# Flag 2 summed behind the fourth chunk, tile 2 normalised by GpSimd, and new orders for every engine

## The chip, the core and the metric

One core of a Trainium2 chip runs the whole program. The metric is the device time of one execution in microseconds. The kernel before was timed three times: 368.39, 368.41 and 369.13 us, median 368.41.

## The reference, cut to what matters

The input is 16 sequences of 256 tokens with 128 features, 4096 tokens. It goes through a feed-forward block (FFN), an attention-like block, and the same FFN again, each with a residual.

```
ln(x)  = (x - mean) / sqrt(var + 1e-5)                 # over the 128 features
ffn(x) = h = silu(x @ w1.T * s1) * (x @ w2.T * s2)     # 128 -> 512, weights of -1, 0, 1
         h = gelu(h @ h1.T * sh1); h = gelu(h @ h2.T * sh2)   # 512 -> 512, exact gelu
         return h @ w3.T * s3                          # 512 -> 128
att(x) = h = ln(x) * gamma + beta
         keys = h @ Wk.T + bk; values = h @ Wv.T + bv
         w = exp((keys @ Wka.T + bka) / sqrt(128)); w = w / cumsum(w)   # along the sequence
         return cumsum(w * keys) * values
x = x + 0.5 * ffn(ln(x));  x = x + att(ln(x));  x = x + 0.5 * ffn(ln(x))
```

## The kernel before, in words

**Tiles and stages.** The 4096 tokens are 8 tiles of 512. Each FFN works on each tile, so there are 16 tiles of FFN work: T = 0 to 7 are the first FFN, 8 to 15 the second, and a0 to a7 are the attention of a tile. Activations stand with features on partitions and the 512 tokens along the free axis. In the order strings, p1.m is hidden chunk m (of 4) of w1 and w2 (two banks of PSUM: "gate" and "up"), p2.m and p3.m are chunk m of h1 and h2, p4 is w3. tanh, gate and up form the gated product of chunk m; high1, high2 and high3 round an activation to a high part, low1, low2 and low3 form the remainder; gelu2 and gelu3 belong to p2 and p3. Each product is made twice, with the high and with the low part, as one weight block of 128x128 against 512 columns: 16 matmuls for p1 of a tile, 32 for p2, 32 for p3, 8 for p4.

**Orders.** START, SECOND_LAYER and STEPS (lines 27 to 186) hold, for each engine, the order of its instructions, written out by hand. Each step of STEPS is one tile; AHEAD (line 193) says how many tiles ahead of the step an item without a number works; "2:t" is item t of tile 2. Engines meet through semaphores alone: every instruction waits for the counts that it needs, and what stands behind it in its engine's order waits with it.

**Flags.** The weights are exact in the high format if their low bits are zero. DVE and ACT reduce the low bits of each part of the weights (items bits:...), raise_flag gathers them (line 1015), TensorE sums them over the partitions with a one-column matmul (flag_sum, line 750), copy_flag brings the sum to SBUF as an integer (line 1024), and TensorE loads it into a register and takes one of two copies of the following instructions (lines 851 to 860). Flag 1 (w1, w2) stands ahead of p1 of tile 0; flag 2 (h1) ahead of the second layer of tile 0; flag 3 (h2, w3) ahead of the rest. Before, flag 2 is summed between p1.1 and p1.2 of tile 0 in the bank y_ps, and p1.3, which writes that bank, waits for its copy (line 684). In the second layer of tile 0 (p2_first, line 698) the products run chunk by chunk of their input (a, b, c, d), hi and lo, into four banks at once, as the inputs come.

**Norms.** Tiles 0 to 2 (BY_PE, line 189) are normalised with the tokens on partitions: DVE takes statistics (norm_stats, norm_aggr, norm_veps), GpSimd takes the root (norm, line 575), ACT writes z (z_blocks), and TensorE turns z by four transposes (item t on PE, line 785) into PSUM. ACT and DVE read it from there as xn_hi and xn_lo. The other tiles are normalised "over columns": DVE takes the statistics, GpSimd aggregates them (aggregate, line 533) into a small tile of means and roots, SyncE's queue writes it to memory (park, line 488) and reads it back broadcast to all partitions in two transfers (wide, line 497), and GpSimd adds and multiplies the tile's columns (xn_add and xn_mult, items xn.0 and xn.1). TensorE isn't needed for it.

**Loads.** SyncE's queue issues the weights and the first tiles' x, waits for h2 and w3, then loads x of tiles 2 to 7 (x_sb), four attention weights, and xt, the transposed input, in one transfer (lines 481 to 486).

Of the kernel before, what the change touches and what calls it, by code (L numbers as in the profile page):

```python
# [29 lines left out]
        "p1.0 p1.1 flag:sum2 p1.2 p1.3",  # L30
    ),
    "ACT": (
        "hi:w1 hi:w2 z",
        "t vec:s1 bits:h1.1 bits:h1.3 tanh.0 tanh.1 tanh.2 high1.0 tanh.3 high1.1 z.0 z.1 high1.2 bits:h2.0 "
        "high1.3 1:t",
    ),
    "DVE": (
        "stats aggr veps bits:w1 bits:w2 norm",
        "flag:copy1 bits:h1.0 t vec:scales bits:h1.2 stats flag:raise2 aggr gate.0 veps flag:copy2 up.0 gate.1 "
        "up.1 low1.0 gate.2 up.2 gate.3 up.3 bits:h2.1 low1.3 1:t",  # L40
# [11 lines left out]
        "",  # L52
        "park wide",
        "a0:park a0:wide park wide",
        "a1:park park a1:wide wide",
        "park wide",
        "a2:park park a2:wide wide",
# [5 lines left out]
        "a6:park 8:store a6:wide park wide",  # L63
        "a7:park a7:wide 9:store park wide",
        "10:store park 11:store wide store",
# [4 lines left out]
        "norm",  # L70
        "norm xn.0 xn.1",
        "a0:norm norm a0:xn.0 a0:xn.1 xn.0 xn.1",
        "a1:norm norm a1:xn.0 a0:weight a1:xn.1 xn.0 xn.1",
        "norm a0:dt xn.0 xn.1",
        "a2:norm a1:weight norm a2:xn.0 a2:xn.1 a1:dt xn.0 xn.1",
        "a3:norm norm a3:xn.0 a3:xn.1 a2:weight xn.0 xn.1",
        "a2:dt norm a4:norm xn.0 xn.1",
        "a3:weight norm a4:xn.0 a4:xn.1 xn.0 xn.1",
        "a5:norm a3:dt a4:weight a5:xn.0 a5:xn.1 norm a4:dt xn.0 xn.1",
# [68 lines left out]
    ),  # L148
    "DVE": (
# [36 lines left out]
}  # L186

POOL_FIRST = ("norm", 1, 2)
BY_PE = (0, 1, 2)
AGGREGATE = 3  # L190
LINES = 4

# [4 lines left out]
def macaron_block(nc, x, xt, w1t, w2t, h1t, h2t, w3t, wkt, wkat, wvt, wkn, vecs, out, seq):  # L197
# [10 lines left out]
    with ExitStack() as ctx:  # L208
# [219 lines left out]
        def flag_home(part):  # L428
            return (hid_ps[0], y_ps, xt_ps)[part - 1][0:1, 0:1]
# [93 lines left out]
        def _(eng):  # L523
# [79 lines left out]
            for k in range(MC):  # L603
                hi("h2", k)
# [613 lines left out]
```

## Time and profile before

| what | value |
|---|---|
| median of three runs | 368.41 us |
| the profiled execution's own time | 368.15 us |
| its span, first to last instruction | 366.4 us |
| TensorE's mean granted clock | 0.998 |
| busy: TensorE, DVE, ACT, GpSimd | 98%, 86%, 77%, 45% |
| read and written | 18.36 and 2.18 MB |

Times in the rows are microseconds from the start of the span. PE is TensorE, DVE VectorE, ACT ScalarE, POOL GpSimd, and SPq the transfers that SyncE issues. A timeline row gives the start, the busy time, the engine, the line, the operation, output<-input, the shapes and, in brackets, the idle time before it and what ended it. The end of a matmul is modelled: a 512-column matmul shows 0.39 us while the next one starts 0.23 us behind it.

### The profile page before, as it was taken

What the parts mean: (1) busy time and instruction counts of PE and PEld (TensorE: products, weight loads), DVE (VectorE), ACT (ScalarE), POOL (GpSimd) and SP (SyncE); (2) the same over time, 40 slices, a digit from 0 to 9 for tenths busy, and PEclk for the clock granted to TensorE, in tenths of its full rate; (3) what the DMA queues carried; (4) which work ended last, traced back from release to release, by engine and by line L of the source; (5) the groups of instructions that cost most, each with busy time, mean ns of one, the idle gap of its engine ahead of it and who ended that gap; (6) DMA issues with size and microseconds to landing.
All of it is one profiled execution on the core that took longest, in us unless ns stands there. A gap on an engine that the chain in (4) does not pass through costs nothing.

```text
span 366.4 us, 5194 instructions
## 1 busy us (share of the span) xinstructions
PE 359.3 (98%) x1578; PEld 285.1 (78%) x1578; DVE 316.2 (86%) x550; ACT 283.1 (77%) x465; POOL 163.3 (45%) x251
## 2 busy tenths in 40 slices
PE   7999999999999999999999999999999999999996
PEld 2678888787877777788778787787778777888885
DVE  5999688999989998889899989998899799857642
ACT  4998777987777879776887968877897697686763
POOL 3553344649045565812685545652573740530000
PEclk9999999999999999999999999999999999999999
DMA  7770103030100301300222012012022020040001
GB/s 245 270 294 4 54 3 107 8 110 9 58 2 0 86 29 36 83 0 2 59 59 59 1 59 59 0 59 86 0 59 88 2 86 2 4 111 2 1 30 63
DMA packets 16256, 20.94 MB, mean 57 GB/s; under 512 B 7008, under 2 KB 8288, under 8 KB 15968
## 3 DMA queue, kind: packets, MB, share of 16 engines
q1 hardware_dynamic: 15504, 19.75, 18.2%
q10 hardware_dynamic: 720, 0.80, 0.7%
q8 instruction: 16, 0.26, 0.3%
q14 instruction: 16, 0.13, 0.1%
HBM read 18.36 MB, written 2.18 MB: 56 GB/s over the span
## 4 chain that ended last, share of the span: by engine, by line
PE 96%; DVE 2%; issue 1%; ACT 1%; POOL 0%; POOLq 0%; ACTq 0%
PE hid_ps L643 62%; PE gate_ps L643 8%; PE y_ps L643 8%; PE up_ps L643 7%; PE y_ps L662 2%; PE xt_ps L829 2%; PE xt_ps L833 2%; PE xt_ps L836 2%; PE y_ps L843 1%; PE gate_ps L707 1%; PE up_ps L707 1%; DVE gate L1070 0%; PE xt_ps L643 0%; DVE xt_sb L1142 0%; PE xt_ps L656 0%
## 5 line engine op out<-in xcount | busy, mean ns | idle before, releaser
L643 PE MATMUL hid_ps<-act_hi,hi_h 128*128 128x512 f32 x480 | 193.3, 403 | 0.0
L643 PE MATMUL hid_ps<-act_lo,hi_h 128*128 128x512 f32 x480 | 186.7, 389 | 0.0
L1092 DVE TENSOR_TENSOR act_lo<-full,act_hi 128x512 fp32r<-128x512 f32 x185 | 132.8, 742 | 23.6 <-ACT act_hi L909 20.6
L902 ACT ACTIVATE full<-hid_ps,vec 128x512 f32<-128x512 f32 x123 | 84.1, 687 | 57.2 <-PE hid_ps L643 51.7
L643 PEld LDWEIGHTS hid_ps<-act_hi,hi_h 128*128 128x128 f32 x480 | 90.3, 188 | 22.8 <-issue 2.6
L643 PEld LDWEIGHTS hid_ps<-act_lo,hi_h 128*128 128x128 f32 x480 | 90.2, 188 | 21.3 <-issue 2.6
L909 ACT ACTIVATE act_hi<-full 128x512 fp32r<-128x512 f32 x127 | 78.6, 628 | 1.6
L567 POOL TENSOR_TENSOR xnt<-xt_sb,wide 128x512 f32<-128x512 f32 x21 | 29.4, 1400 | 45.8 <-DMA wide<-rows 45.8
L885 ACT ACTIVATE tanh<-gate_ps,s_half 128x512 f32<-128x512 f32 x60 | 40.4, 680 | 7.4 <-PE gate_ps L643 7.3
L1070 DVE SCALAR_TENSOR_TENSOR gate<-tanh,gate_ps 128x512 f32<-128x512 f32 x60 | 40.3, 674 | 6.5 <-ACT tanh L885 6.4
L1082 DVE SCALAR_TENSOR_TENSOR full<-up_ps,s_half,gate 128x512 f32<-128x512 f32 x60 | 44.1, 741 | 1.1
L890 ACT ACTIVATE act_hi<-full 128x512 fp32r<-128x512 f32 x60 | 36.9, 625 | 1.9 <-DVE full L1082 1.7
L573 POOL TENSOR_TENSOR xnt<-xnt,wide 128x512 f32<-128x512 f32 x21 | 30.0, 1428 | 3.2 <-POOL xnt L567 0.4
L622 POOL TENSOR_TENSOR xt_sb<-xt_sb,adelta 128x512 f32<-128x512 f32 x8 | 12.3, 1532 | 42.7 <-DVE adelta L1174 42.7
L540 POOL TENSOR_TENSOR pair_diff<-stats 128x4 f32<-128x4 f32 x21 | 8.2, 388 | 44.2 <-DVE stats L1040 44.2
L1158 DVE RECIPROCAL rcsum<-csum 128x256 f32<-128x256 f32 x16 | 27.8, 1740 | 0.0
L553 POOL TENSOR_TENSOR pair<-veps,half 128x4 f32<-128x4 f32 x21 | 26.1, 1244 | 3.3 <-POOL veps L550 0.4
L643 PE MATMUL gate_ps<-xn_hi,hi_w 128*128 128x512 f32 x59 | 25.1, 425 | 0.3 <-ACT full L902 0.3
L643 PE MATMUL y_ps<-act_hi,hi_w 128*128 128x512 f32 x60 | 23.8, 396 | 0.0
L643 PE MATMUL y_ps<-act_lo,hi_w 128*128 128x512 f32 x60 | 23.4, 390 | 0.0
L643 PE MATMUL gate_ps<-xn_lo,hi_w 128*128 128x512 f32 x59 | 23.0, 391 | 0.0
L643 PE MATMUL up_ps<-xn_hi,hi_w 128*128 128x512 f32 x59 | 23.0, 390 | 0.0
(170 smaller groups left out, 440.3 us busy)
## 6 DMA issues: line engine op xcount, KB each, us to landing
wide<-rows SPq DMA_DIRECT2D x42, 256.0 KB, 3.7
xt_sb<-xt SPq DMA_DIRECT2D x1, 2048.0 KB, 10.6
out<-xt_sb SPq DMA_DIRECT2D x7, 256.0 KB, 4.0
x_sb<-x SPq DMA_DIRECT2D x1, 1536.0 KB, 6.8
raw_h<-h2t SPq DMA_DIRECT2D x4, 256.0 KB, 7.1
raw_h<-h1t SPq DMA_DIRECT2D x2, 256.0 KB, 6.1
rows<-pair SPq DMA_DIRECT2D x21, 4.0 KB, 2.2
raw_w<-w2t ACTq DMA_DIRECT2D x1, 256.0 KB, 4.0
```

The costliest lines, as they stand in the source:

```text
L553: eng.tensor_tensor(pair_b[q][:, 1, :], veps[:, :], half[:, :], ALU.pow).then_inc(s_pow, 1)
L567: eng.tensor_tensor(xnt_b[i][:, :], xt_tile(t), wide_b[i][:, 0:TOK], ALU.add).then_inc(s_centred, 1)
L573: eng.tensor_tensor(xnt_b[i][:, :], xnt_b[i][:, :], wide_b[i][:, TOK:2 * TOK], ALU.mult).then_inc(s_xn, 1)
L643: mm = eng.matmul(ps, w, a, start=(first and n == 0), stop=(last and n == len(seq_) - 1))
L885: eng.activation(tanh_b[m % 2][:, :], gate_home(T, m)[:, :], ACT.Tanh, scale=s1_half[:, m:m + 1]).then_inc(s_tanh, 1)
L890: eng.activation(act_hi[first_act(T)][:, m, :], full1[m % 2][:, :], ACT.Copy).then_inc(s_hi[1], 1)
L902: eng.activation(full23[m % 2][:, :], home23(n, T, m)[:, :], ACT.Gelu, scale=col("sh1" if n == 2 else "sh2", m)).then_inc(s_gelu[n], 1)
L909: eng.activation(act_hi[n][:, m, :], full23[m % 2][:, :], ACT.Copy).then_inc(s_hi[n], 1)
L1070: eng.scalar_tensor_tensor(gate_b[m % 2][:, :], tanh_b[m % 2][:, :], 1.0, gate_home(T, m)[:, :], ALU.add, ALU.mult).then_inc(s_gate, 1)
L1082: eng.scalar_tensor_tensor(full1[m % 2][:, :], up_home(T, m)[:, :], s12_half[:, m:m + 1], gate_b[m % 2][:, :], ALU.mult, ALU.mult).then_in ...
L1092: eng.tensor_tensor(act_lo[a][:, m, :], full[m % 2][:, :], act_hi[a][:, m, :].bitcast(F32), ALU.subtract).then_inc(s_lo[n], 1)
L1158: eng.reciprocal(rcsum[:, b], csum[:, b]).then_inc(s_rc, 1)
```

## The change

Flag 2: its sum moves behind p1.3 of tile 0 into the bank gate_ps[0], and waits for gate.0 instead of xn_lo. p1.3 no longer waits for the copy. Tile 2 leaves BY_PE: its four transposes, z and root are gone, and it is normalised over columns. Its rows and its columns of xt get transfers of their own with two semaphores, ahead of the rest. On GpSimd the casts of h2 and w3 become items of the order, three casts of h2 ahead of tile 2's aggregation, the fourth behind it, w3 behind xn.1. All orders are written anew. On ACT the reductions of h1's bits move from ahead of tanh.0 to between the tanhs. In the diff below the steps 2 to 15 of each engine, which hold the same items as before in other orders, are left out.

```diff
 START:
     "PE": (
         "flag:sum1 t",
-        "p1.0 p1.1 flag:sum2 p1.2 p1.3",
+        "p1.0 p1.1 p1.2 p1.3 flag:sum2",
     "ACT": (
-        "hi:w1 hi:w2 z",
-        "t vec:s1 bits:h1.1 bits:h1.3 tanh.0 tanh.1 tanh.2 high1.0 tanh.3 high1.1 z.0 z.1 high1.2 bits:h2.0 "
-        "high1.3 1:t",
+        "hi:w1 hi:w2 z 0:t vec:s1",
+        "tanh.0 tanh.1 bits:h1.1 tanh.2 bits:h1.3 bits:h2.0 high1.0 tanh.3 high1.1 z.0 high1.2 z.1",
     "DVE": (
-        "stats aggr veps bits:w1 bits:w2 norm",
-        "flag:copy1 bits:h1.0 t vec:scales bits:h1.2 stats flag:raise2 aggr gate.0 veps flag:copy2 up.0 gate.1 "
-        "up.1 low1.0 gate.2 up.2 gate.3 up.3 bits:h2.1 low1.3 1:t",
+        "stats aggr veps bits:w1 bits:w2 norm flag:copy1 0:t bits:h1.0 vec:scales",
+        "bits:h1.2 gate.0 stats up.0 aggr flag:raise2 gate.1 flag:copy2 veps up.1 low1.0 gate.2 up.2 gate.3 "
+        "up.3 2:stats low1.3 1:t bits:h2.1 bits:h2.2 flag:raise3 1:gate.0 flag:copy3 1:up.0 0:low2.0 0:low2.1 "
+        "1:gate.1 1:up.1 3:stats 0:low2.2 0:low2.3 1:gate.2 1:low1.0 1:up.2",
 SECOND_LAYER:
-    "p2ahi.0 p2ahi.1 p2ahi.2 p2ahi.3 p2alo.1 p2alo.3 p2bhi.3 p2alo.0 p2alo.2 p2bhi.0 p2bhi.2 t p2blo.0 p2bhi.1 "
-    "p2blo.1 p2blo.3 p2chi.0 p2blo.2 p2clo.0 p2dhi.0 p2chi.1 p2chi.2 p2clo.1 p2dlo.0 p2chi.3 p2dhi.1 p2clo.3 "
-    "p2clo.2 p2dlo.1 flag:sum3 p1.0 p2dhi.2 p2dhi.3 p1.1 p2dlo.2 p2dlo.3"
+    "p2ahi.2 p2ahi.1 p2ahi.3 p2alo.2 p2alo.3 p2alo.1 p2ahi.0 p2bhi.0 p2bhi.1 p2bhi.2 p2alo.0 p2blo.1 p2blo.0 "
+    "p2chi.0 p2chi.1 p2blo.2 t p2clo.1 p2clo.3 p2dhi.1 p2clo.0 p2dhi.0 p2chi.2 p2dlo.0 p2dhi.3 p1.0 p2bhi.3 "
+    "p2dlo.1 p2clo.2 p2blo.3 p2dhi.2 flag:sum3 p2chi.3 p2dlo.2 p2dlo.3 p1.1"
 STEPS, steps 0 and 1:
     "SP": (
-        "",
+        "park wide",
     "POOL": (
-        "norm",
-        "norm xn.0 xn.1",
+        "hi:h2.0 hi:h2.1 hi:h2.2 norm hi:h2.3 xn.0 xn.1",
+        "hi:w3 norm xn.0 xn.1",
     "PE": (
-        "p1.2 p1.3 fold p3.0 p3.1",
-        "t 0:p3.2 p1.0 0:p3.3 p2.0 p1.1 p2.1 p2.2 p2.3 p4 p1.2 p1.3 a0:u p3.0 p3.1 p3.2 p3.3",
+        "p1.2 fold p1.3 p3.0 p3.1 p3.2 p3.3",
+        "p1.0 p1.1 p2.0 p2.1 p4 p2.2 p2.3 p1.2 a0:u p1.3 p3.0 p3.1 p3.2 p3.3",
     "ACT": (
-        "bits:w3 bits:h2.3 gelu2.0 high2.0 gelu2.1 tanh.0 high2.1 tanh.1 gelu2.2 gelu2.3 high2.2 high1.0 "
-        "high2.3 high1.1 tanh.2 z gelu3.0 tanh.3 2:t high3.0 gelu3.1 high1.2 high3.1 gelu3.2 high1.3 high3.2 "
-        "gelu3.3 high3.3",
+        "0:high1.3 bits:w3 t bits:h2.3 gelu2.0 tanh.0 gelu2.1 high2.0 high2.1 tanh.1 gelu2.2 gelu2.3 high2.2 "
+        "tanh.2 high2.3 tanh.3 high1.0 high1.1 gelu3.0 gelu3.1 high1.2 high3.0 2:t high3.1 gelu3.2 high3.2 "
+        "2:tanh.0 high1.3 gelu3.3 high3.3",
     "DVE": (
-        "bits:h2.2 flag:raise3 stats low2.0 flag:copy3 aggr gate.0 veps low2.1 gate.1 up.0 up.1 low2.2 low2.3 "
-        "fold low1.0 gate.2 3:stats up.2 low1.1 2:t gate.3 up.3 low3.0 low1.2 low3.1 low1.3 low3.2 low3.3",
+        "low1.1 gate.3 low3.0 2:t up.3 low3.1 low1.2 low1.3 2:gate.0 low3.2 fold",
...
-BY_PE = (0, 1, 2)
-AGGREGATE = 3
+BY_PE = (0, 1)
+AGGREGATE = 2
...
+        s_x2t, s_xt2 = sem("s_x2t"), sem("s_xt2")
...
-        norm_of = {("ffn", t): t for t in range(2)}
-        for i, order in enumerate(STEPS["DVE"]):
+        norm_of = {}
+        for i, order in enumerate(START["DVE"] + STEPS["DVE"], -2):
...
-            return (hid_ps[0], y_ps, xt_ps)[part - 1][0:1, 0:1]
+            return (hid_ps[0], gate_ps[0], xt_ps)[part - 1][0:1, 0:1]
...
-            xload(2, NT, s_xr)
+            xload(2, 3, s_x2t)
+            eng.dma_start(xt_tile(2), xt[:, 2 * TOK:3 * TOK]).then_inc(s_xt2, 16)
+            xload(3, NT, s_xr)
             for dst, src in ((wk, wkt), (wka, wkat), (wv, wvt), (wk_rows, wkn)):
                 eng.dma_start(dst[:, :], src).then_inc(s_watt, 16)
-            eng.dma_start(xt_sb[:, :], xt).then_inc(s_xt, 16)
+            eng.dma_start(xt_sb[:, 0:2 * TOK], xt[:, 0:2 * TOK]).then_inc(s_xt, 16)
+            eng.dma_start(xt_sb[:, 3 * TOK:], xt[:, 3 * TOK:]).then_inc(s_xt, 16)
...
-            for k in range(MC):
-                hi("h2", k)
-            hi("w3", 0)
-
...
-                if (T, m) in ((0, 3), (1, 1)):
-
-                    eng.wait_ge(s_flag, T + 2)
+                if (T, m) == (1, 1):
+
+                    eng.wait_ge(s_flag, 3)
...
                 if part == 2:
-                    eng.wait_ge(s_xlo_half, 2)
+                    eng.wait_ge(s_gate, 1)
```

xn_add waits for s_xt2 for tile 2 and for both other transfers of xt (32) for the rest; stats waits for s_x2t for tile 2; the first dt waits for 32.

## Rows read from the trace of the kernel before

**Rows 1.** The page: busy time of each engine over the span.

```profile
PE 359.3 (98%) x1578; PEld 285.1 (78%) x1578; DVE 316.2 (86%) x550; ACT 283.1 (77%) x465; POOL 163.3 (45%) x251
```

**Rows 2.** The chain of waits: by line, and pieces (start, us, what).

```profile
by line: PE hid_ps L643 61.8%; PE gate_ps L643 7.7%; PE y_ps L643 7.6%; PE up_ps L643 7.1%; PE y_ps L662 2.1%; PE xt_ps L833 1.9%; PE xt_ps L829 1.9%; PE xt_ps L836 1.9%; PE y_ps L843 1.5%; PE gate_ps L707 0.9%; PE up_ps L707 0.9%; issue 0.
...
316.63 14.51 PE hid_ps L643 x64
```

**Rows 3.** Timeline, TensorE (start, busy, line, what, idle before).

```profile
8.69 0.36 PE L678 MATMUL gate_ps<-xn_hi,hi_w 128*128 128x256 f32 x1 [0.56 <-ACT xn_hi L968]
...
10.42 0.40 PE L643 MATMUL up_ps<-xn_lo,hi_w 128*128 128x512 f32 x1
11.10 0.19 PE L764 MATMUL y_ps<-ones,inexact 128*1 128x1 f32 x2 [0.29 <-DVE inexact L1022]
...
13.64 0.47 PE L707 MATMUL gate_ps<-act_hi,hi_h 128*128 128x512 f32 x1 [0.22 <-ACT act_hi L890]
...
25.50 0.47 PE L643 MATMUL gate_ps<-xn_hi,hi_w 128*128 128x512 f32 x1 [0.32 <-ACT full L902]
...
26.86 0.49 PE L643 MATMUL hid_ps<-act_hi,hi_h 128*128 128x512 f32 x1
...
30.63 0.60 PE L656 MATMUL xt_ps<-ident,z 128*128 128x128 f32 x4
...
31.30 0.39 PE L643 MATMUL hid_ps<-act_lo,hi_h 128*128 128x512 f32 x1
...
358.20 0.28 PE L643 MATMUL gate_ps<-act_hi,hi_w 128*128 128x256 f32 x1
...
362.26 0.59 PE L747 MATMUL xt_ps<-full,raw_w 128*128 128x256 f32 x2
```

**Rows 4.** Timeline, VectorE (DVE), the opening.

```profile
7.58 0.15 DVE L1027 CAST flag_i<-hid_ps 1x1 int32<-1x1 f32 x1 [0.30 <-PE hid_ps L756]
...
10.12 0.87 DVE L1040 BATCH_NORM_STATS2 stats<-x_sb 128x6 f32<-128x128 f32 x4
...
11.32 0.66 DVE L1070 SCALAR_TENSOR_TENSOR gate<-tanh,gate_ps 128x512 f32<-128x512 f32 x1
...
12.11 0.73 DVE L1082 SCALAR_TENSOR_TENSOR full<-up_ps,s_half,gate 128x512 f32<-128x512 f32 x1
```

**Rows 5.** Timeline, ScalarE (ACT), the opening.

```profile
8.88 0.63 ACT L914 ACTIVATE keys<-raw_h 128x512 f32<-128x512 uint16 x1 [0.18 <-DMA raw_h<-h1t]
...
9.66 0.63 ACT L914 ACTIVATE csum<-raw_h 128x512 f32<-128x512 uint16 x1
...
10.29 1.25 ACT L885 ACTIVATE tanh<-gate_ps,s_half 128x512 f32<-128x512 f32 x2
...
12.87 0.63 ACT L890 ACTIVATE act_hi<-full 128x512 fp32r<-128x512 f32 x1
```

**Rows 6.** Timeline, GpSimd (POOL), 18 to 42 us.

```profile
18.27 2.76 POOL L584 CAST hi_h<-raw_h 128x512 fp32r<-128x512 f32 x4
...
30.02 0.21 POOL L540 TENSOR_TENSOR pair_diff<-stats 128x4 f32<-128x4 f32 x1 [4.71 <-DVE stats L1040]
...
38.73 1.29 POOL L567 TENSOR_TENSOR xnt<-xt_sb,wide 128x512 f32<-128x512 f32 x1 [5.62 <-DMA wide<-rows]
40.17 1.56 POOL L573 TENSOR_TENSOR xnt<-xnt,wide 128x512 f32<-128x512 f32 x1
```

**Rows 7.** Timeline, SyncE's queue of transfers.

```profile
16.05 0.45 SPq L486 DMA_DIRECT2D xt_sb<-xt  x1
33.14 0.39 SPq L495 DMA_DIRECT2D rows<-pair  x1
34.73 0.34 SPq L503 DMA_DIRECT2D wide<-rows  x1
```

**Rows 8.** DMA issues (count, KB each, median us from issue to landing).

```profile
xt_sb<-xt SPq DMA_DIRECT2D x1, 2048.0 KB, 10.6
```

**Rows 9.** Windows, TensorE: busy, PEclk (granted clock), DMA share, GB/s.

```profile
365.00:365.50 0.50, 0.00 (x0) 0.50 0.75 262
```

More of the change, by code:

```diff
@@ L51 @@
     "SP": (
-        "",
+        "park wide",
         "park wide",
         "a0:park a0:wide park wide",
-        "a1:park park a1:wide wide",
-        "park wide",
-        "a2:park park a2:wide wide",
+        "a1:park a1:wide park",
+        "park 5:wide wide",
+        "a2:park a2:wide park wide",
         "a3:park a3:wide park wide",
@@ L62 @@
         "park wide",
-        "a6:park 8:store a6:wide park wide",
-        "a7:park a7:wide 9:store park wide",
-        "10:store park 11:store wide store",
+        "a6:park a6:wide park wide",
+        "a7:park a7:wide park 8:store wide",
+        "park 9:store 10:store 11:store wide store",
         "store",
@@ L69 @@
     "POOL": (
-        "norm",
-        "norm xn.0 xn.1",
+        "hi:h2.0 hi:h2.1 hi:h2.2 norm hi:h2.3 xn.0 xn.1",
+        "hi:w3 norm xn.0 xn.1",
         "a0:norm norm a0:xn.0 a0:xn.1 xn.0 xn.1",
[L73 to L79, printed above, removed]
+        "a1:norm norm 6:norm a1:xn.0 a0:weight a1:xn.1 xn.0 xn.1",
+        "a0:dt a1:weight xn.0 xn.1",
+        "a2:norm norm a2:xn.0 a2:xn.1 xn.0 a1:dt xn.1",
+        "a3:norm norm a3:xn.0 a2:weight a3:xn.1 xn.0 xn.1",
+        "a2:dt norm a4:norm a3:weight xn.0 xn.1",
+        "norm a4:xn.0 a4:xn.1 a3:dt xn.0 xn.1",
+        "a5:norm a4:weight a5:xn.0 a5:xn.1 norm a4:dt xn.0 xn.1",
         "norm a5:weight xn.0 xn.1",
@@ L562, in xn_add @@
                     eng.wait_ge(s_x1, t + 1)
+                elif t == 2:
+                    eng.wait_ge(s_xt2, 16)
                 elif t < NT:
-                    eng.wait_ge(s_xt, 16)
+                    eng.wait_ge(s_xt, 32)
                 else:
@@ L602, in _ @@
                     low1(stage)
-            for k in range(MC):
-                hi("h2", k)
-            hi("w3", 0)
             def emit(stage, chunk, t):
-                if stage in ("norm", "att_norm"):
+                if stage == "hi":
+                    hi(t, chunk or 0)
+                elif stage in ("norm", "att_norm"):
                     kind = "ffn" if stage == "norm" else "att"
@@ L796, in emit @@
                             return
-                        free("xt", (s_xlo, t))
-                        transpose4(xt_ps, z, s_t)
                     elif stage == "p4":
@@ L1107, in emit @@
                 elif stage == "stats":
-                    if t <= 2:
-                        eng.wait_ge((s_x0, s_x1t, s_xr)[t], 16)
+                    if t <= 3:
+                        eng.wait_ge((s_x0, s_x1t, s_x2t, s_xr)[t], 16)
                     norm_stats("ffn", t)
@@ L1145, in emit @@
                     if t == 0:
-                        eng.wait_ge(s_xt, 16)
+                        eng.wait_ge(s_xt, 32)
                     eng.wait_ge(s_p4, t + 1)
```

162 rows, old and new, of the table STEPS are left out of this document.

## The prediction

> **What bounds the kernel now.** I read the busy line of the page first, then the chain of waits, then TensorE's timeline of the opening, then those of the engines that feed it. TensorE is busy 359.3 of 366.4 us [rows 1], and the chain of waits is its own stream of matmuls nearly throughout [rows 2]. Its idle time lies at the two ends; in the opening it waits 0.56 us at 8.69, 0.29 at 11.10, and 0.32 at 25.50 [rows 3]. So the change can pay only by what it takes off TensorE's stream and by how it shifts the opening. In between little is to be had: from 26.86 (first p3 matmul of tile 0 [rows 3]) to the first half-width matmul of the last p4, at 358.20 [rows 3], 331.3 us pass. The work in it is 1328 matmuls of 512 columns at 14.51/64 = 0.2267 us [rows 2], 301.1 us; attention's three products and the turned rows, 1.9+1.9+1.9+2.1% of the span [rows 2], 28.6 us; and one tile's four transposes, 0.44. Together 330.1, so 1.2 us of slack.
>
> **Term 1, tile 2's transposes.** They go: from 30.63 to 31.30 pass 0.67 us, in which one ordinary matmul (0.23) lies too [rows 3]. That is -0.44 us on the path, certain in size (bounds -0.3 and -0.6, the duration of the four in their row).
>
> **Term 2, flag 2.** Before, its one-column sum stands between p1.1 and p1.2, and copy and branch run under p1.2 and p1.3; the second layer starts at 13.64, 0.14 after its first input (12.87 + 0.63 = 13.50 [rows 5]). After, the sum is last, and the branch waits right behind it, with nothing on TensorE to cover it. Step by step:
> - TensorE reaches the sum early: p1.1's last matmul starts at 10.42 [rows 3], p1.2 and p1.3 are 8 more at 0.235 (26.86 to 30.63 is 16 of them [rows 3]), done at 12.5.
> - The sum needs raise2, which needs the bits of h1.1 and h1.3. ACT does these now behind tanh. tanh.0 runs while p1.1 does; tanh.1 starts when its bank is written, two matmuls ahead of 10.42, 9.95 + 0.40 = 10.35 [rows 3], and ends at 10.98 (1.25 for two [rows 5]); bits h1.1 0.78 (8.88 to 9.66 [rows 5]), 11.76; tanh.2 0.63, 12.4; bits h1.3, 13.1.
> - DVE has then done bits h1.2, gate.0 (from 10.66, 0.66), stats of tile 1 (0.87), up.0 (0.73) and the aggregation, by about 13.0 [rows 4]; raise2 (0.14, as the copies' 0.15) ends at 13.25; the sum 0.19 [rows 3], 13.45. gate.1 stands ahead of the copy: 0.66, 13.9, and the copy 0.15: 14.0.
> - From the copy's end to the first matmul behind the branch pass 8.69 - 7.73 = 0.96 us at flag 1 [rows 3, 4]. There xn_hi is also waited for, but an input costs 0.14 above, so the branch is what came last; the bounds are 0.14 and 0.96 plus what a longer jump takes. I take 0.96: the second layer starts at 14.9. If the branch were free, high1.0 would hold it: bits h2.0 (0.78) and the copy (0.63) from 13.1 [rows 5] give 14.5 + 0.14 = 14.65.
>
> So the second layer starts 1.25 us later (bounds +1.0 and +1.6). Part of it comes back. Before, from 13.64 to the wait's end at 25.50 go 11.86 us into 44 matmuls of 0.235 (10.35), four transposes (0.44) and the third sum (0.2): 0.9 us of that was waiting for inputs that come chunk by chunk. These inputs are only 0.4 to 0.9 us later than before (low1.0 15.3, high1.2 17.3, low1.3 19.4 by the same durations), so from 14.9 on TensorE meets each of them ready. Its p1.1 of tile 1 starts after 36 matmuls, transposes and sum: 14.9 + 8.46 + 0.64 = 24.0. That bank's first product is done at 24.6; tanh.1, gelu2.2 and gelu2.3 follow on ACT in that order, 3 x 0.63: 26.5, and p1.3 waits for the last, + 0.14. p1.3 then ends and p3.0 starts at 27.6, against 26.86 [rows 3]. **Term 2 is +0.7 us** (bounds +0.2, if all waits in the second stretch go, and +1.3).
>
> The Trainium skill, "Runtime: NRT & Kernel Launch", section "Instruction fetch mechanics", says that a taken branch whose target lies outside the prefetched window stalls for a fetch. The trace agrees in kind (the 0.96 us at flag 1); it gives no price, and by it this jump, over a longer unused copy, could only be dearer.
>
> **Term 3, tile 2's norm by GpSimd.** It needs: the load of tile 2's columns and rows, two transfers more, ahead of the rest (the same bytes in all, and two issues of about 0.45 us on SP's queue [rows 7], hidden by the load itself); stats on DVE behind up.3, about 18.7; GpSimd free of low1 at 18.7, then three casts of h2 at 2.76/4 = 0.69 [rows 6], 20.8; the aggregation, 33.14 - 30.02 = 3.1 [rows 6, 7], 23.9. The fourth cast of h2 moves behind it (24.6), needed at 27.6; that of w3 behind xn.1, needed by p4 near 40: both free. The parking of means and roots leads to the broadcast 34.73 - 33.14 = 1.6 later, and that to xn.0 38.73 - 34.73 = 4.0 later; xn.0 and xn.1 take 41.73 - 38.73 = 3.0 [rows 6, 7]. Sum 23.9 + 8.6 = 32.5. But SP's queue still carries the load of xt, which landed at 16.05 + 10.6 = 26.65 [rows 7, 8]. If the parked rows wait for it, the broadcast is issued at about 27.1 instead of 25.5, and xn.1 ends at 34.1. ACT and DVE then need 0.6 and 0.7 for xn_hi and xn_lo (the copy of rows 5 and the up of rows 4), 34.7 and 35.4. TensorE wants them at 27.6 + 32 x 0.23 = 35.0 and 35.2. So this costs 0 without the queueing and 0.2 with it; the bounds are 0 and 2 (the transfers' own spread). While ACT waits for xn in its order, gelu3.2 and high3.2 of tile 1 stand behind, needed only by p3 later. I take **+0.2**. What goes on DVE (aggregation and veps, 0.4) and ACT (tile 2's z) costs nothing, as neither holds TensorE there.
>
> The Trainium skill, "DMA: Bandwidth & Descriptors", section "Queues, rings and completion order", has each engine take up a queue's descriptors in ring order. By it the 0.2 holds; by free overtaking it is 0. No row here shows a small transfer behind a large one.
>
> **Term 4, the new orders.** From p1.0 of tile 2 on the same matmuls stand in other orders. Before, TensorE never waits there, and its slack is 1.2 us, so I put it at 0 with bounds of -1.0 and +1.5 (a gelu or a low that comes behind two others instead of one, 0.7 each, at two places). The last tile's orders differ by one swap on ACT and DVE, with TensorE's unchanged: 0.
>
> **Sum.** -0.44 + 0.7 + 0.2 + 0 = +0.5 on the profiled execution's 368.15, 368.6; the median of the runs was 0.26 above that execution. Between +0.3 and +0.5 over 368.41 I say 368.8 us, since each duration was taken whole although neighbours overlap by 0.05.
>
> **Rivals.**
> - *The opening gains and the orders pack better.* For it: the wait at 25.50, the slack of 1.2 us. Term 2 at +0.2, no wait for tile 2, and 0.7 to 1.0 of slack gone: -0.44 + 0.2 - 0.9 = -1.1, 367.3. Against: the input chain behind flag 2 alone sets 14.65. Chance 0.24.
> - *Slower: tile 2's normalised columns come late.* Place: p1.0 of tile 2, about 35. It decides once xn.1 ends behind 34.4; each microsecond more is one on the path. For it: the load of xt ends in the middle of the parking, and the 1.6 and 4.0 were read from a queue with nothing else in it. Price 1.3: 370.1. Chance 0.14.
> - *The clock.* After its last matmul (362.26, ending 362.85 [rows 3]) TensorE's granted clock fell to 0.5, the 1.2 GHz level, by 365.0 [rows 9]. The changed kernel idles 0.8 and 1.45 us around the sum. If it falls, 3 us of work at that level cost 1.5: 370.3. Against: two gaps, each shorter than the 2.1 us between that end and that fall. Chance 0.07.
> - *An order starves TensorE once or twice* in the long stretch: +1.0, 369.8. Chance 0.13.
> - The forecast: 0.42, its own range 368.1 to 369.5.
>
> **Numbers.** What a measurement of this kernel can tell from no change is about 0.2%, 0.74 us: faster is under 367.67, slower above 369.15. Faster: the first rival's 0.22. Within: 0.34 of the forecast and 0.06 of the others' edges. Slower: 0.08 of the forecast and 0.30 of the others. The range, 367.1 to 370.8, leaves a tenth on either side.
>
> **What would show it.** Second layer's first matmul near 14.9 with the flag's copy some 1 us before it; if it stands at 13.9 or before, term 2 failed. raise2 near 13.1, ended by ACT's bits. p3.0 of tile 0 near 27.6. xn.1 of tile 2 ending 32.5 to 34.1, and p1.0 of tile 2 with a wait under 0.3. No idle of TensorE from there to 358. A clock under 1.00 between 12 and 20 would prove the third rival. A gap before p1.0 of tile 2 of over 1 us proves the second.

## The result and the profile after

The changed kernel took 369.77 us (median of 20 runs) against 368.46 for the kernel before: 1.3 us slower, ratio 1.0038 with a 95% interval of 1.0029 to 1.0046. The forecast was 368.8, in a range of 367.1 to 370.8, with 0.38 on slower; the time lies in the range and above the forecast. The profiled execution is the fastest of the changed kernel's runs, 368.68 us with a span of 366.9; the kernel before had 368.15 and 366.4. So the first profile shows 0.5 of the 1.3 us, and the rest has to be looked for in other executions. One execution of the kernel before took 518.5 us and is left out of the ratio.

The busy line of its page, beside that in [rows 1], has TensorE at 359.0 us of 366.9. It has four records fewer (the transposes) and 0.3 us less work, and its idle time grew from 7.1 to 7.9 us:

```profile
PE 359.0 (98%) x1574; PEld 284.6 (78%) x1574; DVE 316.3 (86%) x543; ACT 281.8 (77%) x461; POOL 170.9 (47%) x259
```

TensorE's timeline of the changed kernel, lines as in [rows 3]; the steps of the sum can be checked one by one:

```profile
8.89 0.35 PE L684 MATMUL gate_ps<-xn_hi,hi_w 128*128 128x256 f32 x1 [0.60 <-ACT xn_hi L972]
...
13.37 0.19 PE L770 MATMUL gate_ps<-ones,inexact 128*1 128x1 f32 x2 [0.55 <-DVE inexact L1026]
14.60 0.47 PE L713 MATMUL gate_ps<-act_hi,hi_h 128*128 128x512 f32 x1 [1.04 <-ACT act_hi L894]
...
27.47 0.39 PE L649 MATMUL hid_ps<-act_hi,hi_h 128*128 128x512 f32 x1
...
34.73 0.39 PE L649 MATMUL gate_ps<-xn_hi,hi_w 128*128 128x512 f32 x1
34.95 0.47 PE L649 MATMUL gate_ps<-xn_lo,hi_w 128*128 128x512 f32 x1
```

The second layer starts at 14.60 (forecast 14.9, before 13.64), p3.0 of tile 0 at 27.47 (forecast 27.6, before 26.86), and the four transposes of [rows 3] near 30.63 are gone. p1.0 of tile 2 is at 34.73; its second matmul shows 0.47 instead of 0.39 us, and 0.31 to the next: xn_lo came just in time.

What feeds it, in the same kernel's timelines. VectorE gathers flag 2 and copies it:

```profile
13.16 0.16 DVE L1026 TENSOR_REDUCE inexact<-bits 128x1 f32<-128x6 f32 x1
...
13.83 0.14 DVE L1031 CAST flag_i<-gate_ps 1x1 int32<-1x1 f32 x1
```

ScalarE's bits of h1.3, and high1.0:

```profile
12.40 0.63 ACT L918 ACTIVATE csum<-raw_h 128x512 f32<-128x512 uint16 x1
...
13.63 0.62 ACT L894 ACTIVATE act_hi<-full 128x512 fp32r<-128x512 f32 x1
```

GpSimd's first aggregation step for tile 2, xn.0 and xn.1:

```profile
20.90 0.20 POOL L546 TENSOR_TENSOR pair_diff<-stats 128x4 f32<-128x4 f32 x1
...
30.30 1.29 POOL L575 TENSOR_TENSOR xnt<-xt_sb,wide 128x512 f32<-128x512 f32 x1 [6.17 <-DMA wide<-rows]
31.73 1.56 POOL L581 TENSOR_TENSOR xnt<-xnt,wide 128x512 f32<-128x512 f32 x1
```

SyncE's queue, park and wide of tile 2:

```profile
23.58 0.39 SPq L501 DMA_DIRECT2D rows<-pair  x1
27.13 0.34 SPq L509 DMA_DIRECT2D wide<-rows  x1
```

The gathering stands at 13.16 (forecast 13.1), 0.13 us behind ScalarE's bits. The row at 14.60 names high1.0, but that is done at 14.25, and the flag's copy at 13.97 with the branch behind it. An input costs 0.14 us by the forecast's reading, which gives 14.39, so the branch came last, 0.63 us behind the copy. xn.1 ends at 33.29 (forecast 32.5 to 34.1). The broadcast is issued 3.55 us behind the park, against 1.6 in [rows 7]. That 1.6 is near the shortest of its kind: over the 22 parks of the changed kernel's first profile the time from issue to landing is 1.5 us at least, 2.5 in the median and 4.2 at most, so the forecast took a low value from one row.

### The profile page after: what moved, and what is told of

It reads as the page before. It is cut to its first block, busy times and chain, and to the rows that moved or that the text cites. A ratio compares the mean times of both kernels' runs of the same rounds, so it can differ in the third digit from the quotient of the medians.

```text
span 366.9 us, 5192 instructions
## 1 busy us (share of the span) xinstructions
PE 359.0 (98%) x1574; PEld 284.6 (78%) x1574; DVE 316.3 (86%) x543; ACT 281.8 (77%) x461; POOL 170.9 (47%) x259
## 4 chain that ended last, share of the span: by engine, by line
PE 93%; DVE 2%; ACT 2%; issue 1%; POOL 0%; POOLq 0%; ACTq 0%
PE hid_ps L649 60%; PE gate_ps L649 7%; PE y_ps L649 7%; PE up_ps L649 7%; PE y_ps L668 2%; PE xt_ps L840 2%; PE xt_ps L837 2%; PE xt_ps L833 2%; PE y_ps L847 2%; PE gate_ps L713 1%; DVE act_lo L1096 1%; PE up_ps L713 1%; ACT tanh L889 1%; DVE full L1086 0%; ACT full L906 0%
## 5 line engine op out<-in xcount | busy, mean ns | idle before, releaser
L1096 DVE TENSOR_TENSOR act_lo<-full,act_hi 128x512 fp32r<-128x512 f32 x185 | 134.4, 752 | 21.3 <-ACT act_hi L913 17.3
L575 POOL TENSOR_TENSOR xnt<-xt_sb,wide 128x512 f32<-128x512 f32 x22 | 31.7, 1440 | 46.5 <-DMA wide<-rows 46.5
L581 POOL TENSOR_TENSOR xnt<-xnt,wide 128x512 f32<-128x512 f32 x22 | 31.0, 1407 | 3.0 <-POOL xnt L575 0.4
L649 PE MATMUL gate_ps<-xn_hi,hi_w 128*128 128x512 f32 x59 | 25.9, 438 | 0.0
L649 PE MATMUL up_ps<-xn_lo,hi_w 128*128 128x512 f32 x59 | 23.0, 391 | 0.0
```

The costliest lines, as they stand in the source:

```text
L575: eng.tensor_tensor(xnt_b[i][:, :], xt_tile(t), wide_b[i][:, 0:TOK], ALU.add).then_inc(s_centred, 1)
L581: eng.tensor_tensor(xnt_b[i][:, :], xnt_b[i][:, :], wide_b[i][:, TOK:2 * TOK], ALU.mult).then_inc(s_xn, 1)
L649: mm = eng.matmul(ps, w, a, start=(first and n == 0), stop=(last and n == len(seq_) - 1))
L1096: eng.tensor_tensor(act_lo[a][:, m, :], full[m % 2][:, :], act_hi[a][:, m, :].bitcast(F32), ALU.subtract).then_inc(s_lo[n], 1)
```

## The experiments

All ratios are to the kernel before on the same chip, five rounds each. "Room" is the time from the end of ScalarE's copy of a normalised tile (h_t or xn_hi) to the first matmul that reads it. In the places where TensorE was held, the room was 0.14 or 0.15 us for xn_hi and 0.06 for h_t: that is the time of one hand-over. A room that is only a little larger holds nothing.

My theory after the result was that tile 2's columns come late in most executions (the second rival). The rival theory was that the new orders of the long stretch cost it, which the forecast had at 0.

### The changed kernel again, and its two halves

> The changed kernel once more, as the measure for the three beside it. Every theory: ratio to the kernel before 1.003 to 1.005. Its new profile is one more draw: theory 'tile 2 late' expects a wait at p1.0 of tile 2 (near 34.7) that differs from the first profile's 0.08 us; theory 'orders' expects no such wait, but idle time of TensorE somewhere between 40 and 358.

> START, SECOND_LAYER and steps 0 and 1 of the changed kernel (flag 2 behind the 4th chunk, tile 2 by GpSimd), steps 2 to 15 with the orders of the kernel before (gelu3.3, low3.2 and low3.3 of tile 1 moved over the border). Theory 'the opening costs it' (flag 2's branch +0.6 and tile 2's late columns, less 0.44): ratio 1.003 to 1.004, as the changed kernel. Theory 'orders' (the steady orders cost most of the 1.3 us): 1.000 to 1.001.

> The kernel before with the new orders of steps 2 to 15 alone; opening, flag 2 and tile 2's norm as before. Theory 'the opening costs it': ratio 1.000 within 0.001. Theory 'orders': 1.002 to 1.003, with TensorE idle or stretched near 125 to 136, where VectorE has no idle time.

The edits exchange whole steps of the orders, for example on TensorE in step 11:

```diff
-        "p1.0 p1.1 p4 p2.0 a6:logits u p2.1 p2.2 a7:u a6:keys p2.3 p1.2 p3.0 p1.3 a6:values p3.1 p3.2 p3.3",
+        "p1.0 p1.1 p4 p2.0 a6:logits u p2.1 a7:u p2.2 a6:keys p2.3 p1.2 a6:values p1.3 p3.0 p3.1 p3.2 p3.3",
```

| kernel | us | ratio | interval |
|---|---|---|---|
| changed, again | 370.15 | 1.0043 | 1.0028 to 1.0059 |
| new opening, old steps 2 to 15 | 369.26 | 1.0009 | 0.9995 to 1.0022 |
| old opening, new steps 2 to 15 | 369.70 | 1.0029 | 1.0018 to 1.0040 |

The halves add up to the whole. The opening with tile 2 costs 0.3 us, with an interval that includes no change at all, and the new orders of the long stretch 1.1 us (0.0029 x 368.6), clear of the noise. My first theory fell. The second profile of the changed kernel has a span of 368.1 us, 1.2 more than the first. Of these, 0.5 us pass before p1.0 of tile 0 (9.38 against 8.89), which is an accident of the execution, as it is the same kernel. The rest lies behind it, mainly at tile 15's p1.0, where 0.83 us are lost. The first fence is its list of waits of TensorE (who waited, for whom, us in total, times, longest), the second its timeline at tile 15's p1.0:

```profile
PE gate_ps L649 <- ACT xn_hi L965: 0.3, 1, 0.3
PE gate_ps L649 <- DVE xn_lo L1131: 0.2, 1, 0.2
```

```profile
332.38 0.47 PE L649 MATMUL gate_ps<-xn_hi,hi_w 128*128 128x512 f32 x1 [0.26 <-ACT xn_hi L965]
333.02 0.50 PE L649 MATMUL gate_ps<-xn_lo,hi_w 128*128 128x512 f32 x1 [0.16 <-DVE xn_lo L1131]
```

In the profile of the kernel before, p1.0 of tile 15 doesn't wait. In the profile of the new steps on the old opening the wait is somewhere else, at attention tile 6's logits:

```profile
263.39 1.12 PE L788 MATMUL xt_ps<-h_t,wl 128*128 128x512 f32 x2 [0.93 <-ACT h_t L931]
```

ScalarE's h_t there:

```profile
262.52 0.81 ACT L931 ACTIVATE h_t<-xnt,vec 128x512 f32<-128x512 f32 x1 [2.58 <-POOL xnt L528]
```

VectorE's reciprocal, and the statistics of that tile, there:

```profile
243.84 1.75 DVE L1113 RECIPROCAL rcsum<-csum 128x256 f32<-128x256 f32 x1
246.01 1.49 DVE L1047 TENSOR_TENSOR act_lo<-full,act_hi 128x512 fp32r<-128x512 f32 x1 [0.42 <-ACT act_hi L864]
247.42 0.88 DVE L995 BATCH_NORM_STATS2 stats<-y_ps 128x6 f32<-128x128 f32 x4
```

and the same two instructions in the kernel before (VectorE's reciprocal and statistics, ScalarE's h_t):

```profile
242.82 1.74 DVE L1158 RECIPROCAL rcsum<-csum 128x256 f32<-128x256 f32 x1
244.82 0.89 DVE L1040 BATCH_NORM_STATS2 stats<-y_ps 128x6 f32<-128x128 f32 x4 [0.26 <-PE y_ps L662]
```

```profile
260.12 0.81 ACT L976 ACTIVATE h_t<-xnt,vec 128x512 f32<-128x512 f32 x1
```

The turned rows of attention tile 6 are on TensorE at 244.15 before and at 244.57 here. VectorE takes their statistics 0.67 us later before, and 2.85 us later here: the new order puts low2.1 (the act_lo row) ahead of them, which waits for ScalarE. h_t is ready at 260.93 before, 0.99 us ahead of its logits at 261.92; here it is ready at 263.33, and the logits start 0.06 us later, after 0.93 us of idle time. It is the only profile with these steps whole in which tile 6 holds TensorE. In the second of the changed kernel its room is 0.16, and the logits follow the matmul before them without a gap (262.56 and 262.79).

Two things shorten tile 15's room. Its rows are turned at 314.15 before and at 316.04 in the second profile of the changed kernel, and from there to p1.0, the 0.42 us lost at the wait taken off, TensorE has 15.9 us of work instead of 16.8. And on SyncE's queue three stores stand between its park and its wide (the changed kernel's second profile; after it the kernel before):

```profile
321.16 0.37 SPq L501 DMA_DIRECT2D rows<-pair  x1
321.58 1.43 SPq L519 DMA_DIRECT2D out<-xt_sb  x3
324.56 0.33 SPq L509 DMA_DIRECT2D wide<-rows  x1
```

```profile
319.10 0.37 SPq L495 DMA_DIRECT2D rows<-pair  x1
319.51 0.47 SPq L513 DMA_DIRECT2D out<-xt_sb  x1
320.70 0.32 SPq L503 DMA_DIRECT2D wide<-rows  x1
```

The wide leaves 3.4 us behind the park instead of 1.6; in the first profile of the same kernel it is 2.7. In the profile of the new steps on the old opening, with the same three stores, it is 1.94:

```profile
321.75 0.37 SPq L450 DMA_DIRECT2D rows<-pair  x1
322.17 1.43 SPq L468 DMA_DIRECT2D out<-xt_sb  x3
323.69 0.40 SPq L458 DMA_DIRECT2D wide<-rows  x1
```

The room of the tightest norms in each profile follows, with TensorE's time in two parts: up to p1.0 of tile 0, and from there to the first half-width matmul of the last p4 (358.20 in [rows 3]). All in us:

| profile | span | attention 6 | tile 15 | p1.0 starts | to the last p4 |
|---|---|---|---|---|---|
| before | 366.4 | 0.99 | 1.66 | 8.69 | 349.51 |
| changed, first | 366.9 | 0.59 | 0.58 | 8.89 | 349.98 |
| changed, second | 368.1 | 0.16 | 0.14 | 9.38 | 350.74 |
| new opening, old steps | 367.2 | 0.99 | 1.67 | 8.87 | 350.35 |
| new steps, old opening | 367.9 | 0.06 | 0.69 | 9.03 | 350.72 |

The spans alone mislead: up to 0.7 us of their differences lies ahead of p1.0 of tile 0, and the start of p1.0 scatters as much between profiles of kernels with the same orders up to there. The last column is the one to compare, and each number of it is one execution.

A third place is VectorE's. In the first profile of the changed kernel a p3 product of tile 5 is late for its input: 0.45 us pass at 135.69 where 0.23 should. VectorE did attention's scan there ahead of low2.0 and low2.1, and ScalarE's gelu waited 2.28 us for them. Four of the eight profiles with these steps lose this third of a microsecond, the second of the changed kernel not. The rows:

```profile
135.69 0.39 PE L649 MATMUL hid_ps<-act_hi,hi_h 128*128 128x512 f32 x1
136.14 0.50 PE L649 MATMUL hid_ps<-act_lo,hi_h 128*128 128x512 f32 x1
```

VectorE before that:

```profile
128.29 1.26 DVE L1170 TENSOR_TENSOR_SCAN pooled<-ones,wgt_keys 128x256 f32<-128x256 f32 x2
129.48 2.32 DVE L1096 TENSOR_TENSOR act_lo<-full,act_hi 128x512 fp32r<-128x512 f32 x2
```

ScalarE's gelu:

```profile
131.28 0.69 ACT L906 ACTIVATE full<-hid_ps,vec 128x512 f32<-128x512 f32 x1 [2.28 <-DVE act_lo L1096]
```

### Which steps

> The kernel before with the new orders of steps 2 to 8 alone (the border items with them). The whole of steps 2 to 15 cost 1.0029. In two profiles of the new orders TensorE was held near 135.7 by VectorE's scan ahead of low2.0 (0.3 us). Theory 'VectorE's new places in the middle': ratio 1.001 to 1.002 here. Theory 'late norms at the end': 1.000 here.

> The kernel before with the new orders of steps 9 to 15 alone. Theory 'late norms at the end' (attention tile 6 near 262, and tile 15 near 332, behind three stores): ratio 1.002 to 1.003, and a wait of TensorE in the profile at 262 or 332. Theory 'VectorE's new places in the middle': 1.001 or less.

> The kernel before with the new orders of steps 2 to 12 alone. In the profiles so far the room between attention tile 6's h_t and the logits that need it is 0.99 us before and 0.06 to 0.59 with the new orders; between tile 15's xn_hi and its p1.0 it is 1.66 before and 0.14 to 0.7 with them. Steps 2 to 8 alone cost 1.0008, all 1.0029. Theory 'two late norms': here tile 15 has its 1.66 again and tile 6 stays short, so the ratio lies between, 1.0015 to 1.0025. If tile 15 alone is the cost: 1.0008.

The edits are again whole steps, with the items that cross the border moved. Those of the three on TensorE in step 9, where the first two meet (old in steps 2 to 8, new in the two others):

```diff
-        "p1.0 8:p3.3 p2.0 p4 p2.1 u p1.1 a4:values p2.2 p2.3 p1.2 p1.3 a5:logits p3.0 12:u p3.1 a5:keys p3.2 p3.3",
+        "p1.0 8:p3.3 p1.1 p2.0 p4 p2.1 u a4:values p2.2 p2.3 p1.2 p1.3 a5:logits p3.0 p3.1 12:u a5:keys p3.2 p3.3",
```

Measured: steps 2 to 8 alone 369.21 us, 1.0008 (0.9999 to 1.0017), a little under the 1.001 to 1.002 of the one theory and over the 1.000 of the other. So by subtraction the new steps 9 to 15 hold most of the 1.1 us, some 0.8; no run shows this share by itself. Steps 9 to 15 alone gave 377.25 us, 1.0226 (1.0212 to 1.0240), and steps 2 to 12 alone 369.82 us, 1.0035 (1.0022 to 1.0049). Both lie above what was expected, but both are spoilt by where I divided the orders, as their waits show. Steps 9 to 15 (the list of waits):

```profile
PE y_ps L617 <- DVE xt_sb L1103: 4.4, 1, 4.4
...
PE xt_ps L788 <- ACT h_t L931: 1.4, 1, 1.4
```

Steps 2 to 12:

```profile
PE y_ps L617 <- POOL xt_sb L577: 0.8, 1, 0.8
```

In the former, a turn of rows waits 4.4 us for VectorE at the border, which neither of the two whole orders has. In the latter, the turn of tile 15's rows waits 0.75 us because a reciprocal of attention tile 7 had to cross the border. Tile 6's room is 0.17 and tile 15's 1.66 there, as expected, but the time says nothing on their shares.

### The stores between park and wide

> The new orders of steps 2 to 15 on the opening before (1.0029), with one thing changed: on SyncE's queue the stores no longer stand between the park and the wide of tiles 14 and 15. Expected: wide of tile 15 is issued 1.6 to 2.0 us behind its park instead of 2.7 to 3.4, tile 15's p1.0 doesn't wait. If the stores are the main cost the ratio falls to 1.001; if it is one of three places, to 1.002.

```diff
-        "a7:park a7:wide park 8:store wide",
-        "park 9:store 10:store 11:store wide store",
+        "a7:park a7:wide park wide 8:store",
+        "9:store 10:store park wide 11:store store",
```

> The kernel before with three stores between park and wide of tile 15, as in the changed kernel, and nothing else. The wide is issued about 1.1 to 1.8 us later, which tile 15's room of 1.66 us just holds: the room falls to 0 to 0.6. Theory 'margin': ratio 1.000 to 1.001, while the same placement on a shorter margin costs. If stores on the queue cost by themselves: 1.002.

```diff
-        "a7:park a7:wide 9:store park wide",
-        "10:store park 11:store wide store",
+        "a7:park a7:wide park wide",
+        "park 9:store 10:store 11:store wide store",
```

The first gave 369.99 us, 1.0035 (1.0024 to 1.0046), where the same kernel without the edit had 1.0029: no gain. The wide left 1.6 us behind the park again, but in the kernel that was edited it had stood at 1.94 already and not at the 2.7 to 3.4 of the changed kernel, so the edit took off only 0.3 us. Tile 15's room went from 0.69 to 0.85. TensorE lost time at three other places: 0.34 us at 135 and 0.5 at 260 for a low part of VectorE's, and 0.4 at 304 for a gelu of ScalarE's. The second gave 368.45 us, 1.0001 (0.9992 to 1.0009). Its queue:

```profile
319.84 0.37 SPq L495 DMA_DIRECT2D rows<-pair  x1
320.26 1.43 SPq L513 DMA_DIRECT2D out<-xt_sb  x3
321.79 0.40 SPq L503 DMA_DIRECT2D wide<-rows  x1
```

Three stores cost 0.35 us there, the same as in the new steps on the old opening, and not the 1.8 of the changed kernel. Tile 15's room stayed at 1.67, where 0 to 0.6 was expected. So both expectations missed on the queue: three stores by themselves delay the wide by a third of a microsecond, which costs nothing on a room of 1.66. The 1.1 to 1.8 us of the changed kernel were neither made nor undone by these two runs. There the queue waited for the park to land after the stores were issued, and why it landed later isn't known. That mending one place leaves the next, because several norms and inputs have little room at once, fits these three places, but it is argued and not shown.

### Flag 2

> The changed kernel with ACT's reductions of h1.1 and h1.3 ahead of tanh.0 again, h2.0's behind high1.0, and on VectorE stats, raise2 and the aggregation ahead of gate.0 and the flag's copy ahead of gate.1. By the sum's term 2 the second layer starts near 13.95 instead of 14.60, and the time falls by 0.3 to 0.6 us against the changed kernel (ratio 1.002 to 1.003). If the inputs of the second layer and not its start set the opening, p3.0 of tile 0 stays at 27.5 and the ratio at 1.004.

```diff
-        "tanh.0 tanh.1 bits:h1.1 tanh.2 bits:h1.3 bits:h2.0 high1.0 tanh.3 high1.1 z.0 high1.2 z.1",
+        "bits:h1.1 bits:h1.3 tanh.0 tanh.1 tanh.2 high1.0 bits:h2.0 tanh.3 high1.1 z.0 high1.2 z.1",
-        "bits:h1.2 gate.0 stats up.0 aggr flag:raise2 gate.1 flag:copy2 veps up.1 low1.0 gate.2 up.2 gate.3 "
+        "bits:h1.2 stats flag:raise2 aggr gate.0 veps up.0 flag:copy2 gate.1 up.1 low1.0 gate.2 up.2 gate.3 "
```

> The kernel before with flag 2's sum behind p1.3 in the bank gate_ps[0], its copy behind up.0 on VectorE, and p1.3 free of the flag; ACT's order, tile 2 and all else as before. By the changed kernel's profile the first matmul behind the branch comes 0.63 us after the copy's end: here 13.05 + 0.63 = 13.7 against 13.64. Expected: ratio 1.000 within 0.0008, the sum's 0.29 us of idle gone and the same amount idle behind it. If the bare branch costs more: 1.001 to 1.002.

```diff
-        "p1.0 p1.1 flag:sum2 p1.2 p1.3",
+        "p1.0 p1.1 p1.2 p1.3 flag:sum2",
-            return (hid_ps[0], y_ps, xt_ps)[part - 1][0:1, 0:1]
+            return (hid_ps[0], gate_ps[0], xt_ps)[part - 1][0:1, 0:1]
-                if (T, m) in ((0, 3), (1, 1)):
-                    eng.wait_ge(s_flag, T + 2)
+                if (T, m) == (1, 1):
+                    eng.wait_ge(s_flag, 3)
-                    eng.wait_ge(s_xlo_half, 2)
+                    eng.wait_ge(s_gate, 1)
```

Executions start p1.0 at slightly different times, so the table counts from there. up.3 is VectorE's last step of the gated product, from which the last inputs of the second layer are rounded:

| kernel | p1.0 starts | to the second layer | to the end of up.3 | to p3.0 of tile 0 |
|---|---|---|---|---|
| before | 8.69 | 4.95 | 8.88 | 18.17 |
| changed | 8.89 | 5.71 | 9.24 | 18.58 |
| flag 2 early | 9.13 | 5.18 | 9.17 | 18.56 |
| flag 2 late alone | 8.38 | 4.87 | 8.98 | 18.23 |

TensorE's timeline with flag 2 early:

```profile
13.00 0.19 PE L770 MATMUL gate_ps<-ones,inexact 128*1 128x1 f32 x2
14.31 0.47 PE L713 MATMUL gate_ps<-act_hi,hi_h 128*128 128x512 f32 x1 [1.12 <-ACT act_hi L894]
...
27.69 0.39 PE L649 MATMUL hid_ps<-act_hi,hi_h 128*128 128x512 f32 x1
```

The early flag moves the second layer's start forward by 0.53 us, and p3.0 doesn't follow. What sets the opening are the inputs behind the start, which come from ScalarE and VectorE: the alternative written down beforehand. In all four kernels p3.0 stands 9.25 to 9.39 us behind the end of up.3, wherever the second layer starts. The time agrees: 370.40 us, 1.0050 (1.0034 to 1.0065), not under the changed kernel's 1.0043. With the late sum alone the kernel before gives 368.56 us, 1.0010 (1.0000 to 1.0020). That is just over the expected 0.0008 and at the lower edge of the alternative, that the bare branch costs more; the interval holds both. VectorE's copy of the flag and the first matmul behind the branch there:

```profile
12.47 0.15 DVE L1027 CAST flag_i<-gate_ps 1x1 int32<-1x1 f32 x1 [0.29 <-PE gate_ps L764]
```

```profile
12.24 0.19 PE L764 MATMUL gate_ps<-ones,inexact 128*1 128x1 f32 x2
13.25 0.47 PE L707 MATMUL gate_ps<-act_hi,hi_h 128*128 128x512 f32 x1 [0.82 <-DVE gate L1070]
```

### Tile 2's transfers

> The changed kernel with the two large transfers of xt issued behind tile 2's park and wide instead of ahead of them, so that these meet an empty queue. Predicted from the first profile: wide issued about 1.6 us behind park instead of 3.55, xn.1 of tile 2 ends near 31.4 instead of 33.3, the wait at p1.0 of tile 2 goes. Theory 'tile 2 late': the time falls by 0.3 to 0.8 us against the changed kernel. Theory 'orders': under 0.2 us.

> The new opening on the steady orders before (1.0009), with the two large transfers of xt issued behind tile 2's park and wide. In the opening's profile tile 2's xn_lo was late by 0.27 us (0.5 with what follows). Expected: that wait goes, the room at p1.0 of tile 2 grows to 1.0 us or more, and the ratio falls to 1.0000 or a little under (0.9995). If tile 2's columns aren't the cost of the opening: 1.0009 as before.

```diff
-        "park wide",
+        "",
...
-            eng.dma_start(xt_sb[:, 0:2 * TOK], xt[:, 0:2 * TOK]).then_inc(s_xt, 16)
-            eng.dma_start(xt_sb[:, 3 * TOK:], xt[:, 3 * TOK:]).then_inc(s_xt, 16)
...
+            park("ffn", 2)
+            wide("ffn", 2)
+            eng.dma_start(xt_sb[:, 0:2 * TOK], xt[:, 0:2 * TOK]).then_inc(s_xt, 16)
+            eng.dma_start(xt_sb[:, 3 * TOK:], xt[:, 3 * TOK:]).then_inc(s_xt, 16)
```

On the whole change: 369.80 us, 1.0031 (1.0019 to 1.0043), against 1.0043. On the new opening with the old steps: 368.59 us, 1.0003 (0.9993 to 1.0013), against 1.0009. Both are lower, by 0.2 to 0.4 us, which neither interval tells from nothing. The wait for tile 2's xn_lo, 0.27 us in the profile of the new opening, is gone in that of its mended form, where the room of tile 2's xn_hi is 0.73 instead of 0.15; 1.0 was expected. But the wide still leaves 2.9 us behind the park in the first of these kernels, and not the expected 1.6, with next to nothing on the queue (a window's columns are its length, PEclk, DMA share, GB/s):

```profile
23.70 0.39 SPq L499 DMA_DIRECT2D rows<-pair  x1
26.64 0.34 SPq L507 DMA_DIRECT2D wide<-rows  x1
```

```profile
22.00:24.00 2.00, 1.00 0.01 4
```

The changed kernel's second profile, with xt ahead of the park, has the same 2.9 us:

```profile
24.05 0.39 SPq L501 DMA_DIRECT2D rows<-pair  x1
26.95 0.34 SPq L509 DMA_DIRECT2D wide<-rows  x1
```

From park to wide pass 3.55, 2.90, 3.82 and 3.68 us in the four profiles with xt ahead, and 2.94 and 3.28 in the two with xt behind. The room of tile 2's xn_hi is 0.71 and 1.12 in the two profiles of the changed kernel itself. So what these two edits seem to gain is within what one kernel shows from one execution to the next, and whether the load of xt holds up the park isn't shown.

## Why the prediction was right or wrong

- **The direction and the range** held: slower had 0.38, same 0.40, and 369.77 is inside. The likeliest value was 1.0 us low, so its own range, to 369.5, was missed. What kept the time inside is the width of the range, which the rivals had opened, and not the sum; in this the prediction was lucky.
- **Term 1, the transposes, -0.44:** they are gone from TensorE's stream; no run prices them alone.
- **Term 2, flag 2, +0.7:** by the profile p3.0 of tile 0 is 0.61 us later, 0.41 of it counted from p1.0. The second layer started at 14.60 instead of 14.9. The first matmul came 0.63 us behind the flag's copy, here and with the late sum alone (12.62 to 13.25), not 0.96. The sum said that the late start costs and that part comes back; the early flag showed that all of the 0.53 us that it moved comes back, and that the orders of ScalarE and VectorE set p3.0. The size was near, the reason only half right.
- **Term 3, tile 2, +0.2:** room 0.71 and 0.08 us of stretch in the first profile, 0.27 us of wait in that of the new opening. The size held. Its reason, the load of xt ahead of the park, isn't shown: with xt behind it the gap was 2.9 and 3.3 us, with xt ahead 2.9 to 3.8. What the sum had wrong is the 1.6 us from park to wide, which was near the shortest on record and not the usual time. Terms 1 to 3 together were to be +0.5; the new opening alone measured +0.3 (-0.2 to +0.8).
- **Term 4, the new orders, 0:** this is the step that failed. The new steps alone measured +1.1 us (0.7 to 1.5), inside its bounds of -1.0 and +1.5 and not at the 0 that went into the sum. The rival that stood for it, "an order starves TensorE once or twice", had 0.13 and named 369.8. I argued that TensorE never waits there before. That was true of the one execution that I had, but it says nothing of how much room each input has: 0.99 us at attention tile 6 and 1.66 at tile 15. The orders themselves show where to look, since the statistics, the turn of rows and the stores move in them.
- **The clock** stayed at 1.00 in every window from 8 to 26 us of the changed kernel's first profile, through both gaps of the opening; that rival fell.

What stays open: how the 0.8 us of steps 9 to 15 divide between attention tile 6, tile 15 and VectorE's places; and why the places change from one execution to the next, so that a first profile can show only 0.5 us in all. The losses seen in the profiles (0.33 to 1.09 us at one to three places each) are of the right size, but no run restored the room of all of them and left the rest of the new orders. That the shrunken rooms are the cause is therefore argued and not shown; that the new orders of steps 2 to 15 cost the time is shown. No version beat the kernel before: the best were 1.0001 and 1.0003.

## What to carry to other kernels

Where an engine is never idle, list the room of each input, not the waits: an order that takes a microsecond of room from several chains at once can show little in one execution and, as this case suggests, cost in the typical one. Compare orders over many runs, and cut them in two to find the half that costs. A start moved forward gains nothing when the inputs behind it come at the same time.

## What the runs showed of the hardware

A parked 4 KB of means and roots landed 1.5 to 4.2 us behind its issue, 2.5 in the median, within one profile of the changed kernel. A sum should take the spread, and not one row. The Trainium skill, "DMA: Bandwidth & Descriptors", section "Queues, rings and completion order", has an engine take descriptors in ring order. By it a large load ahead of the park would hold it up; the runs here show no difference clear of their scatter (2.90 to 3.82 us with the load ahead, 2.94 and 3.28 with it behind), so they neither bear it out nor speak against it.

Three stores in front of the wide cost 0.35 us of issue time in two kernels (1.94 and 1.95 us from park to wide instead of 1.6).

From the end of the copy of a flag to the first matmul behind the branch 0.63 us passed in two kernels (13.97 to 14.60 and 12.62 to 13.25), which is what load and branch cost here when nothing covers them.
